# Attention logits with the features on the partitions: three banks of sums, a product with att two turns behind, edge features as 32 rows of 512

## The chip, the core and the metric

The program runs on one core of one Trainium2 chip. Its time is the device time of one execution in microseconds. Three executions of the kernel before took 2243.04, 2249.6 and 2248.37 us, a median of 2248.37 us. TensorE (PE) does the matrix products, VectorE (DVE) and ScalarE (ACT) work elementwise, GpSimd (POOL) issues gathers whose descriptors it makes itself, SyncE (SP) issues plain transfers.

## The reference, cut to what matters

Four graph layers follow each other over 3125 nodes with 128 features and 103,125 edges sorted by destination. The change touches the last one, an attention layer with 8 heads of 16 channels:

```python
x_l = (x @ W_l).reshape(n, H, C)
x_r = (x @ W_r).reshape(n, H, C)
e = (ea @ W_e).reshape(-1, H, C)
m = jax.nn.leaky_relu(x_l[src] + x_r[dst] + e, NEG_SLOPE)
alpha = jnp.einsum('ehc,hc->eh', m, att)
amax = jax.ops.segment_max(alpha, dst, num_segments=n)
expa = jnp.exp(alpha - amax[dst])
denom = jax.ops.segment_sum(expa, dst, num_segments=n)
a = expa / (denom[dst] + 1e-16)
out = jax.ops.segment_sum(x_l[src] * a[:, :, None], dst, num_segments=n)
```

For each edge there is a logit of each head: three rows of 128 are added, bent at zero (slope 0.2 below it), weighed with att and summed over the 16 channels of a head. Every node has a loop edge with itself, whose edge features are the mean.

## The kernel before, in words

The layer has three stages: `project` makes x_l (stored to memory, and gathered from there) and x_r (kept on chip as `xr`), `attention` goes over the edges, `feed_forward` normalizes and runs the two dense products. The change is in the first two.

`attention` takes the edges in 214 groups of 512 (four tiles of 128, edges on the partitions). There is one turn of the loop per group. The order on each engine is the order of the code; semaphores tie the engines.

- POOL: four gathers for each group (L2112), each of 128 rows of x_l by the edges' sources, into a ring of 28 groups. Before the gathers of group g it waits until group g-6 has been added up (`sums`), and until the ring's place is free.
- SP: two transfers of edge features per group, a broadcast of the destination numbers every second group, and per batch the marks of where nodes begin.
- PE, `logits(g)` (L2118): for each tile e = features times W_e, and x_r by a one-hot matrix `hot` that picks each edge's destination. A row is 136 wide: each head has a 17th column that holds 0.2 times the sum with att, so that the rest needs only max(z, 0) times 0.8 att. Four tiles stand in two banks; two groups take turns.
- DVE, per turn in this order: `one_hots(t+2)` (L2280), `add_rows(t)` (L2287: the sums from PE plus the gathered rows), `weigh(u)` (L2374), `bend(t)` (L2293), `add(u)` of the turn before (L2392), `head_sums(t)` (L2300: the sum over a head's 17 columns, which is alpha).
- A batch is up to 16 groups. When it is over, PE turns the alphas (`turn_alpha`, L2138) so that heads and groups are the partitions and the edges run along the row; DVE scans them for the maximum per node in both directions (L2308), a short chain carries the ends between groups, and the exponentials are turned back as weights.
- From 22 turns behind, group u is summed: DVE multiplies the gathered rows by the weights (`weigh`, output `both`), ACT makes `node_hot` (L2237, L2240), PE multiplies the two (`sum_rows`, L2180), DVE adds the sum into `acc` at a block given by a register. At the end of the loop there are two such groups in some turns, to catch up. At a batch's first group `spread_fall` (L2361, L2362, L2364) makes three short operations ahead of `weigh`.
- In the turns 0 to 4 DVE also computes the loop edges' logits (`own_logits`, L2399), 5 blocks of nodes at a time.

## Time and profile before

| | us |
|---|---|
| median of three runs (lowest, highest) | 2248.37 (2243.04, 2249.6) |
| span of the profiled execution | 2249.7 |
| attention, from the first gather at 984.64 to the last operations near 2187.5 | about 1203 |
| of it gathers, first start 984.64 to last start 2141.25 | 1156.6 |
| after the last gather to the end of attention | about 45 |
| feed_forward | about 62 |

The profile gives the profiled execution's span alone, no time around it; that span lies at the upper end of the three runs, 1.3 us over their median. Busy times over the whole span are PE 1665.0 us (74%), DVE 1504.7 (67%), ACT 969.8 (43%), POOL 916.3 (41%). TensorE's granted clock averages 0.829 of full speed. The share of an engine over the whole span mixes stages: POOL's 41% is nearly all in attention. An operation's row gives its start, its length, the engine, the line, output and inputs; a bracket behind it says how long the engine was idle before it, and what ended that. "issue" stands for idle time for which the profile shows nothing that was waited for.

### The profile page before, as it was taken

What the parts mean: (1) busy time and instruction counts of PE and PEld (TensorE: products, weight loads), DVE (VectorE), ACT (ScalarE), POOL (GpSimd) and SP (SyncE); (2) the same over time, 40 slices, a digit from 0 to 9 for tenths busy, and PEclk for the clock granted to TensorE, in tenths of its full rate; (3) what the DMA queues carried; (4) which work ended last, traced back from release to release, by engine and by line L of the source; (5) the groups of instructions that cost most, each with busy time, mean ns of one, the idle gap of its engine ahead of it and who ended that gap; (6) DMA issues with size and microseconds to landing.
All of it is one profiled execution on the core that took longest, in us unless ns stands there. A gap on an engine that the chain in (4) does not pass through costs nothing. (4 is left out here: it accounts for less than half of the span.)

```text
span 2249.7 us, 34161 instructions
## 1 busy us (share of the span) xinstructions
PE 1665.0 (74%) x10041; PEld 1359.7 (60%) x10041; DVE 1504.7 (67%) x3141; ACT 969.8 (43%) x2263; POOL 916.3 (41%) x880
## 2 busy tenths in 40 slices
PE   5566666899799999865667677766777767776756
PEld 2455555655478887634566666666666656666744
DVE  4766666577744342477677777867777867787875
ACT  0355565677455234430234434434434335344535
POOL 1000000000100000037777777777777777777800
PEclk9555555799999999988788988888888898898877
DMA  2100000000034000034333333333343333333211
GB/s 70 60 1 1 1 1 1 8 0 0 29 87 130 27 1 6 14 100 96 92 90 91 97 93 91 92 96 92 87 100 94 86 95 97 91 93 93 60 39 29
DMA packets 134433, 136.86 MB, mean 61 GB/s; under 512 B 28689, under 2 KB 105074, under 8 KB 134258
## 3 DMA queue, kind: packets, MB, share of 16 engines
q0 software_dynamic: 27776, 60.71, 12.2%
q1 hardware_dynamic: 106482, 73.98, 11.5%
q8 instruction: 90, 1.47, 0.3%
q14 instruction: 85, 0.70, 0.1%
HBM read 129.67 MB, written 4.92 MB: 60 GB/s over the span
## 5 line engine op out<-in xcount | busy, mean ns | idle before, releaser
L2112 POOL DMA_INDIRECT rows<-x_l,src x856 | 896.9, 1048 | 292.5 <-issue 260.1
L2180 PE MATMUL psum<-both,node_hot 128*128 128x144 f32 x1712 | 304.1, 332 | 202.0 <-DVE both L2374 175.2
L2180 PEld LDWEIGHTS psum<-both,node_hot 128*128 128x128 f32 x1712 | 264.7, 222 | 229.4 <-issue 197.4
L2127 PE MATMUL psum<-w_e,edges 128*128 128x272 f32 x856 | 323.9, 466 | 56.7 <-DVE z L2287 46.9
L2129 PEld LDWEIGHTS psum<-x_r,hot 128*128 128x128 f32 x1712 | 313.8, 224 | 51.1
L2129 PE MATMUL psum<-x_r,hot 128*128 x1712 | 313.1, 312 | 0.0
L2287 DVE TENSOR_TENSOR z<-psum,rows 128x544 f32<-128x544 f32 x214 | 154.3, 721 | 235.4 <-issue 163.7
L2237 ACT ACTIVATE apart<-iota,minus_rel 128x128 f32<-128x128 f32 x828 | 261.9, 386 | 0.0
L769 ACT ACTIVATE counts<-psum (+1 forms) x181 | 181.5, 1003 | 175.8 <-PE psum L762 112.1
L1145 POOL TENSOR_TENSOR ht<-ht,mix_rows 128x512 f32<-128x512 f32 (+1 forms) x7 | 7.8, 1149 | 587.4 <-ACT mix_rows L1186 587.4
L1260 PE MATMUL psum<-halves,counts 128*128 128x257 f16 (+1 forms) x1725 | 198.1, 277 | 7.4 <-DVE halves L1465 3.9
L762 PE MATMUL psum<-keys,x 128*128 128x125 f16 x1431 | 201.3, 283 | 0.4
L2127 PEld LDWEIGHTS psum<-w_e,edges 128*128 128x128 f32 x856 | 160.7, 228 | 62.4 <-DVE hot L2280 31.2
L1260 PEld LDWEIGHTS psum<-halves,counts 128*128 128x128 f16 (+1 forms) x1725 | 171.2, 100 | 34.3 <-DVE halves L1465 4.5
L725 DVE TENSOR_TENSOR x<-low_table,c_low 128x2048 f16<-128x2048 f16 x90 | 109.6, 1218 | 116.0 <-PE psum L762 114.6
L762 PEld LDWEIGHTS psum<-keys,x 128*128 128x128 f16 x1431 | 148.3, 104 | 25.8 <-issue 1.6
L2392 DVE TENSOR_TENSOR acc<-acc,psum 128x144 f32 x428 | 128.6, 300 | 44.9 <-PE psum L2180 8.0
L2233 ACT ACTIVATE both<-weight 128x64 f32<-128x64 f32 x214 | 52.9, 247 | 235.7 <-PE psum L2180 232.8
L2300 DVE TENSOR_REDUCE alpha<-z 128x32 f32<-128x544 f32 x214 | 152.5, 713 | 1.5 <-issue 0.3
L2293 DVE SCALAR_TENSOR_TENSOR z<-z,att 128x512 f32<-128x512 f32 x214 | 146.5, 685 | 1.1
L2374 DVE TENSOR_TENSOR both<-rows,weight 128x512 f32<-128x512 f32 x214 | 143.9, 680 | 0.2 <-ACT weight L2224 0.2
L740 PE MATMUL psum<-none 128*128 128x1 f16 x366 | 57.1, 183 | 105.7 <-ACT counts L769 102.1
(335 smaller groups left out, 2187.3 us busy)
## 6 DMA issues: line engine op xcount, KB each, us to landing
rel_row<-e_rel_rows SPq DMA_DIRECT2D x107, 256.0 KB
edges<-edge_t SPq DMA_DIRECT2D x428, 32.0 KB
rows<-x_l,src POOLq DMA_INDIRECT x856
edge_part<-edge_t SPq DMA_DIRECT2D x40, 320.0 KB, 3.1
x_r<-x_l SPq DMA_DIRECT2D x1, 1632.0 KB
ht<-x SPq DMA_DIRECT2D x6, 256.0 KB, 2.8
new<-e_new_before SPq DMA_DIRECT2D x12, 128.0 KB
new<-e_new_behind SPq DMA_DIRECT2D x12, 128.0 KB
```

The costliest lines, as they stand in the source:

```text
L762: last = e.matmul(flat[:, bass.ds(place[i - j * STRIDE], cols)], lows[hot], keys[hot], start=False, stop=True, skip_group_check=True)
L769: return e.activation(counts[:, :, column].rearrange("p h (a j) -> p h a j", j=w), pair.rearrange("p b (a n) -> p (b a) n", n=SLOT)[:, 0:f ...
L1260: last = e.matmul(ps, counts[:, i, b * P:b * P + rows], halves[:, i, :], start=i == 0, stop=i == s.nb - 1)
L2112: e.indirect_dma_start(rows[:, g % ring, j * ROW:(j + 1) * ROW], None, k.xl, bass.IndirectOffsetOnAxis(ap=src[:, at:at + 1], axis=0)).then ...
L2127: e.matmul(pair[:, j // 2, :], edges[:, r, :], w_e[:, j:j + 2, :].rearrange("p j f -> p (j f)"), start=True, stop=False)
L2129: final = e.matmul(pair[:, j // 2, j % 2 * ROW:(j % 2 + 1) * ROW], hot[:, two, j * P:(j + 1) * P], node_rows[j // 2], start=False, stop=j ...
L2180: final = e.matmul(to, near_hot[:, at, j, :], both[:, at, j, :], start=j % 2 == 0, stop=j % 2 == 1)
L2237: e.activation(apart[:, u % 2, j, :], iota[:, :], ACT.Abs, bias=minus_rel[:, 4 * u + j:4 * u + j + 1]).then_inc(*far.up())
L2287: e.tensor_tensor(z[:, g % 2, :].rearrange("p (b f) -> p b f", b=2), pair_of(g), rows_at(g).rearrange("p (b f) -> p b f", b=2), ALU.add).t ...
L2293: e.scalar_tensor_tensor(heads, heads, 0.0, att_of(k, 4), ALU.max, ALU.mult).then_inc(*leaky.up())
L2300: e.tensor_reduce(alpha[:, b.two, :, g - b.first, :], z[:, g % 2, :].rearrange("p (v h c) -> p v h c", v=4, h=HEADS), AX.X, ALU.add).then_ ...
L2374: e.tensor_tensor(both[:, at, :, 0:D].rearrange("p v (h c) -> p v h c", c=CH), rows_at(u).rearrange("p (v h c) -> p v h c", v=4, h=HEADS)[ ...
```

## The change

Within `attention`, the sums are built transposed: features on the partitions, the group's 512 edges along the row, in one bank per group, with three banks in turn (0, 1, 4).

- A row is 128 wide; the 17th columns go, and with them the products that filled them in `project`.
- PE, `begin(g)`: x_r of a block, split into three bf16 parts whose sum is x_r, times the bf16 one-hot matrix (three products of 256 columns for each of the group's two blocks), then W_e (32 x 128) times the edge features (32 rows of 512), one product of 512 columns. `join(g)`: the gathered rows of each tile times the identity, 4 of 128 columns, which adds them transposed. `head_sums(g)`: the bent sums times `att_heads` (att spread over the heads' columns), 512 columns, which gives the alphas with lines on the partitions at once; each group adds its 8 lines into the batch's bank (2 or 3). It runs two turns behind `join` (one at a batch's last group). `turn_alpha` is gone.
- ACT, `slope(g)`: 0.2 times the sums from the bank into `bent`.
- DVE, `bend(g)`: the maximum of the bank and `bent`. `add_rows` and DVE's `head_sums` are gone. `bend` stands behind `add`.
- The bf16 parts of x_r are made by POOL for the first 5 blocks, in `project`, and by DVE for the other 20 in the turns 0 to 3 (four operations for each 5 blocks). `own_logits` moves to the turns 5 to 9 and has one operation more; `add_bias` moves to the turns 10 to 19.
- SP: the edge features of a group go to 32 partitions, in three places instead of six; for group g SP waits for the products of group g-3. Two small loads more, and one smaller one in another form, stand in the tables' loads in `project`; one column more is loaded ahead.
- `hot` and `apart` are bf16.

```diff
-ROW = HEADS * (CH + 1)
+ROW = D
+LINES = 16 * HEADS
...
+                e.memset(k.att_heads[:, :], 0.0).then_inc(*blank.up())
+                e.wait_ge(kept_r.sem, kept_r.at(5))
+                row_parts.split(e, 0, split)
...
+                e.tensor_scalar(k.att_heads[:, LINES - HEADS:LINES], head_of[:, :], cols[:, 2:3], None, ALU.mult).then_inc(*v.up())
...
+class RowParts:
+
+
+    def __init__(self, k, scope, xr, rest):
+        s = k.s
+        self.xr, self.parts = xr, k.sb(scope, "x_r_parts", [P, s.nb, 3, D], BF16)
+        self.rest = rest.rearrange("p (b f) -> p b f", f=D)
+
+    def split(self, e, c, done):
+
+        at, rest = slice(5 * c, 5 * c + 5), self.rest
+        part = [self.parts[:, at, q, :] for q in range(3)]
+        if done.n:
+            e.wait_ge(done.sem, done.at(done.n))
+        e.tensor_copy(part[0], self.xr[:, at, :]).then_inc(*done.up())
+        t = done.n
+        e.wait_ge(done.sem, done.at(t))
+        e.tensor_tensor(rest[:, :, :], self.xr[:, at, :], part[0], ALU.subtract).then_inc(*done.up())
+        t = done.n
+        e.wait_ge(done.sem, done.at(t))
+        e.tensor_copy(part[1], rest[:, :, :]).then_inc(*done.up())
+        t = done.n
+        e.wait_ge(done.sem, done.at(t))
+        e.tensor_tensor(part[2], rest[:, :, :], part[1], ALU.subtract).then_inc(*done.up())
...
-    ring, slots, ahead, deep, lag = RING, 6, 4, 4, 22
+    ring, slots, edge_slots, deep, lag = RING, 6, 3, 4, 22
...
-        edges = sb("edges", [P, slots, P])
-        rel_row, hot = sb("rel_row", [P, slots, 4 * P], I16), sb("hot", [P, 2, 4 * P])
-        z, alpha = sb("z", [P, 2, 4 * ROW]), sb("alpha", [P, 2, 4, 16, HEADS])
+        edges = sb("edges", [DE, edge_slots, 4 * P])
+        rel_row, hot = sb("rel_row", [P, slots, 4 * P], I16), sb("hot", [P, 2, 4 * P], BF16)
+        bent = sb("bent", [P, 3, 4 * P])
...
-        turn_bank, misc = k.bank[4], k.bank[5]
+        split = k.flag("x_r_split")
+        z_banks, misc = (k.bank[0], k.bank[1], k.bank[4]), k.bank[5]
+
+        def summed_in(t):
+
+            ends = [b.over - 1 for b in plan]
+            return [g for g in (t - 2, t - 1) if 0 <= g < groups and (g == t - 1) == (g in ends)]
...
+        def bank_of(b):
+            return k.bank[2 + b.two]
+
+        def alphas_of(b):
+            return bank_of(b)[0:b.lines, :]
...
-                    if old >= 0:
-                        e.wait_ge(products.sem, products.at(old + 1))
+                    if g >= edge_slots:
+                        e.wait_ge(products.sem, products.at(g - edge_slots + 1))
                     for j, at in enumerate(two):
-                        e.dma_start(edges[j * P // 2:(j + 1) * P // 2, r, :], pairs_t[bass.ds(at, 1), :, :]
-                                                    .rearrange("o r e -> (o r) e")).then_inc(*edge_here[r].up(16))
+                        e.dma_start(edges[:, g % edge_slots, j * 2 * P:(j + 1) * 2 * P].rearrange("d (t e) -> d t e", t=2),
+                                    rows_of_pair(at)).then_inc(*edge_here[g % edge_slots].up(16))
...
-                        e.wait_ge(sums.sem, sums.at(g - slots + 1))
+                        e.wait_ge(joined.sem, joined.at(g - slots + 1))
...
-                def logits(g):
-                    r, two, pair = g % slots, g % 2, pair_of(g)
-                    node_rows = [xr[:, bass.ds(block_of.at(2 * g + j), 1), :].rearrange("p o f -> p (o f)") for j in range(2)]
+                def begin(g):
+                    two, z = g % 2, z_banks[g % 3]
+                    blocks = [block_of.at(2 * g + j) for j in range(2)]
+                    due_parts = min(2 * g + 1, s.nb - 1) // 5
+                    if due_parts > min(max(2 * g - 1, 0), s.nb - 1) // 5:
+                        e.wait_ge(split.sem, split.at(4 * due_parts))
                     e.wait_ge(hots.sem, hots.at(g + 1))
-                    e.wait_ge(edge_here[r].sem, edge_here[r].at(2 * lap(g)))
-                    if g >= 2:
-                        e.wait_ge(sums.sem, sums.at(g - 1))
+                    if g >= 3:
+                        e.wait_ge(leaky.sem, leaky.at(g - 2))
+                    for j in range(2):
+                        half = slice(j * 2 * P, (j + 1) * 2 * P)
+                        for q in range(3):
+                            e.matmul(z[:, half], row_parts.parts[:, bass.ds(blocks[j], 1), q, :].rearrange("p o f -> p (o f)"),
+                                     hot[:, two, half], start=j + q == 0, stop=False)
+                    e.wait_ge(edge_here[g % edge_slots].sem, edge_here[g % edge_slots].at(edge_lap(g)))
+                    e.matmul(z, w_e[:, :], edges[:, g % edge_slots, :], start=False, stop=False).then_inc(*products.up())
+
+                def join(g):
+                    z = z_banks[g % 3]
+                    e.wait_ge(got[g % slots].sem, got[g % slots].at(4 * lap(g)))
                     for j in range(4):
-                        if j % 2 == 0:
-                            e.matmul(pair[:, j // 2, :], edges[:, r, :], w_e[:, j:j + 2, :].rearrange("p j f -> p (j f)"),
-                                     start=True, stop=False)
-                        final = e.matmul(pair[:, j // 2, j % 2 * ROW:(j % 2 + 1) * ROW], hot[:, two, j * P:(j + 1) * P],
-                                         node_rows[j // 2], start=False, stop=j % 2 == 1)
-                    final.then_inc(*products.up())
-
-                def turn_alpha(b):
-                    e.wait_ge(alphas.sem, alphas.at(b.over))
+                        final = e.matmul(z[:, j * P:(j + 1) * P], rows_at(g)[:, j * P:(j + 1) * P], k.ident[:, :],
+                                         start=False, stop=j == 3)
+                    final.then_inc(*joined.up())
+
+                def head_sums(g):
+                    b = batch_of(g)
+                    c = g - b.first
+                    low = LINES - HEADS - c * HEADS
+                    e.wait_ge(leaky.sem, leaky.at(g + 1))
+                    if c == 0 and b.i >= 2:
+                        e.wait_ge(weights.sem, weights.at(2 * (b.i - 1)))
+                    e.matmul(alphas_of(b), k.att_heads[:, low:low + b.lines], bent[:, g % 3, :],
+                             start=c == 0, stop=c == b.n - 1).then_inc(*alphas.up())
...
-                logits(0)
+                begin(0)
                 for t in range(len(due)):
+                    if t < groups:
+                        join(t)
+                    for g in summed_in(t):
+                        head_sums(g)
                     if t + 1 < groups:
-                        logits(t + 1)
-                    for piece, turn in ((0, turn_alpha), (1, turn_ends), (2, turn_carries), (5, turn_weights)):
+                        begin(t + 1)
+                    for piece, turn in ((1, turn_ends), (2, turn_carries), (5, turn_weights)):
...
+                def slope(g):
+                    e.wait_ge(joined.sem, joined.at(g + 1))
+                    if g >= 3:
+                        e.wait_ge(alphas.sem, alphas.at(g - 2))
+                    e.activation(bent[:, g % 3, :], z_banks[g % 3], ACT.Copy, scale=NEG_SLOPE).then_inc(*sloped.up())
...
+                        slope(t)
...
-                def add_rows(g):
-                    e.wait_ge(products.sem, products.at(g + 1))
-                    e.wait_ge(got[g % slots].sem, got[g % slots].at(4 * lap(g)))
-                    if g >= 2:
-                        e.wait_ge(alphas.sem, alphas.at(g - 1))
-                    e.tensor_tensor(z[:, g % 2, :].rearrange("p (b f) -> p b f", b=2), pair_of(g),
-                                            rows_at(g).rearrange("p (b f) -> p b f", b=2), ALU.add).then_inc(*sums.up())
-
                 def bend(g):
-                    heads = z[:, g % 2, :].rearrange("p (v h c) -> p v h c", v=4, h=HEADS)[:, :, :, 0:CH]
-                    e.wait_ge(sums.sem, sums.at(g + 1))
-                    e.scalar_tensor_tensor(heads, heads, 0.0, att_of(k, 4), ALU.max, ALU.mult).then_inc(*leaky.up())
-
-                def head_sums(g):
-                    b = batch_of(g)
-                    e.wait_ge(leaky.sem, leaky.at(g + 1))
-                    if b.i >= 2:
-                        e.wait_ge(turned.sem, turned.at(4 * (b.i - 1)))
-                    e.tensor_reduce(alpha[:, b.two, :, g - b.first, :], z[:, g % 2, :].rearrange(
-                        "p (v h c) -> p v h c", v=4, h=HEADS), AX.X, ALU.add).then_inc(*alphas.up())
...
-                        add_rows(t)
                     for u in due[t]:
                         if u in begun:
                             spread_fall(begun[u])
                         weigh(u)
-                    if t < groups:
-                        bend(t)
                     for u in due[t - 1] if t else []:
                         add(u)
                     if t < groups:
-                        head_sums(t)
-                    if t < cuts:
-                        own_logits(t)
-                    if cuts <= t < 3 * cuts:
-                        add_bias(t - cuts)
+                        bend(t)
+                    if t + 1 < cuts:
+                        row_parts.split(e, t + 1, split)
+                    if cuts <= t < 2 * cuts:
+                        own_logits(t - cuts)
+                    if 2 * cuts <= t < 4 * cuts:
+                        add_bias(t - 2 * cuts)```

What now stands on the engines can be read from the compiled order. On DVE, in the middle of the loop, a turn was this before (from the one-hot matrix of a group two ahead, to the next turn's one):

```order
L2280 TENSOR_SCALAR hot<-rel_row,place 128x512
L2287 TENSOR_TENSOR z<-psum,rows 128x544
L2374 TENSOR_TENSOR both<-rows,weight 128x4x128
L2293 SCALAR_TENSOR_TENSOR z<-z,att 128x32x16
L2392 ISA
L2392 TENSOR_TENSOR acc<-acc,psum 128x144
L2392 ISA
L2392 TENSOR_TENSOR acc<-acc,psum 128x144
L2300 TENSOR_REDUCE alpha<-z 128x4x8
```

The same turn on DVE in the changed kernel (2349 is `hot`, 2426 `weigh`, 2444 `add`, 2353 `bend`):

```order
L2349 TENSOR_SCALAR hot<-rel_row,place 128x512
L2426 TENSOR_TENSOR both<-rows,weight 128x4x128
L2444 ISA
L2444 TENSOR_TENSOR acc<-acc,psum 128x144
L2444 ISA
L2444 TENSOR_TENSOR acc<-acc,psum 128x144
L2353 TENSOR_TENSOR bent<-psum,bent 128x512
```

Two operations of the turn are gone. `hot` now stands directly ahead of `both`, and `both` is followed by the additions into `acc`; the bend reads a bank of sums and stands last.

On PE, in the middle of the loop, this is a turn before, `logits` and `sum_rows`:

```order
L2127 MATMUL psum<-w_e,edges 128x272
L2129 ISA
L2129 MATMUL psum<-x_r,hot 128x136 x2
L2127 MATMUL psum<-w_e,edges 128x272
L2129 ISA
L2129 MATMUL psum<-x_r,hot 128x136 x2
L2180 MATMUL psum<-both,node_hot 128x144 x4
```

And in the changed kernel: `join`, `head_sums`, then `begin` with six pairs like the first two rows here, of which the last two pairs are shown, and `sum_rows`, then the next turn's `join` and `head_sums`:

```order
L2174 ISA
L2174 MATMUL psum<-hot,x_r_parts 128x256
L2174 ISA
L2174 MATMUL psum<-hot,x_r_parts 128x256
L2177 MATMUL psum<-edges,w_e 128x512
L2240 MATMUL psum<-both,node_hot 128x144 x4
L2183 MATMUL psum<-ident,rows 128x128 x4
L2194 MATMUL psum<-bent,att_heads 128x512
```

The wait for the gathered rows has moved from DVE's L2287 to PE's L2183, which heads PE's turn.

## Rows read from the trace of the kernel before

**Rows 1.** Busy time in four stretches: the stretch, then each engine; clock, DMA last

```profile
core 0: us, PE busy (x) PEld busy (x) DVE busy (x) ACT busy (x) POOL busy (x), PEclk, DMA share, GB/s
985.00:1110.00 125.00, 73.67 (x304) 60.92 (x304) 90.47 (x140) 7.42 (x20) 96.95 (x93) 0.76 0.41 100
1110.00:1900.00 790.00, 559.77 (x3119) 497.66 (x3120) 589.83 (x1196) 322.98 (x968) 610.09 (x591) 0.87 0.38 93
1900.00:2143.00 243.00, 177.07 (x1024) 158.29 (x1024) 197.50 (x404) 108.67 (x331) 189.46 (x174) 0.87 0.36 89
2143.00:2188.00 45.00, 26.09 (x137) 23.21 (x136) 33.62 (x94) 17.42 (x60) 0.00 (x0) 0.73 0.06 13
```

**Rows 2.** Attention, groups of instructions: count, busy us, mean ns, idle before

```profile
L2112 POOL DMA_INDIRECT rows<-x_l,src x856 | 896.9, 1048 | 292.5 <-issue 260.1 <-DMA x_l<-rows 31.8 <-DVE both L2374 0.6
L2127 PE MATMUL psum<-w_e,edges 128*128 128x272 f32 x856 | 323.9, 466 | 56.7 <-DVE z L2287 46.9 <-DVE hot L2280 9.8
...
L2287 DVE TENSOR_TENSOR z<-psum,rows 128x544 f32<-128x544 f32 x214 | 154.3, 721 | 235.4 <-issue 163.7 <-PE psum L2129 69.4 <-DMA rows<-x_l,src 2.1
L2300 DVE TENSOR_REDUCE alpha<-z 128x32 f32<-128x544 f32 x214 | 152.5, 713 | 1.5 <-issue 0.3
L2293 DVE SCALAR_TENSOR_TENSOR z<-z,att 128x512 f32<-128x512 f32 x214 | 146.5, 685 | 1.1
L2374 DVE TENSOR_TENSOR both<-rows,weight 128x512 f32<-128x512 f32 x214 | 143.9, 680 | 0.2 <-ACT weight L2224 0.2
L2392 DVE TENSOR_TENSOR acc<-acc,psum 128x144 f32 x428 | 128.6, 300 | 44.9 <-PE psum L2180 8.0 <-DVE acc L2392 5.9
...
L2280 DVE TENSOR_SCALAR hot<-rel_row,place 128x512 f32<-128x512 int16 x214 | 104.2, 487 | 5.3 <-PE psum L2129 4.4 <-DMA rel_row<-e_rel_rows 0.9
...
L2224 ACT ACTIVATE weight<-psum 128x512 f32<-128x512 f32 x24 | 13.0, 594 | 6.9 <-PE psum L2160 5.9 <-PE psum L2157 1.0
...
L2347 DVE TENSOR_TENSOR trial<-psum,trial 128x512 f32<-128x512 f32 x12 | 8.3, 691 | 0.4
```

**Rows 3.** The gathers' line: count, shortest/median/longest in ns, first and last start

```profile
L2112 POOL DMA_INDIRECT rows<-x_l,src x856: 940/947/3946, 984.6 to 2141.2; - x172
```

**Rows 4.** In order of time, around 1552 to 1562 us: start, length, engine, operation

```profile
1552.89 0.62 PE L2127 MATMUL psum<-w_e,edges 128*128 128x272 f32 x2
...
1553.35 0.63 PE L2129 MATMUL psum<-x_r,hot 128*128 x4
...
1556.07 0.68 DVE L2374 TENSOR_TENSOR both<-rows,weight 128x512 f32<-128x512 f32 x1
...
1556.57 1.00 POOL L2112 DMA_INDIRECT rows<-x_l,src  x1 [0.31 <-issue]
1556.67 0.68 DVE L2293 SCALAR_TENSOR_TENSOR z<-z,att 128x512 f32<-128x512 f32 x1
...
1561.56 0.68 DVE L2374 TENSOR_TENSOR both<-rows,weight 128x512 f32<-128x512 f32 x1
...
1561.76 1.30 POOL L2112 DMA_INDIRECT rows<-x_l,src  x1 [0.30 <-issue]
```

**Rows 5.** In order of time, first and last of the 18 longest gathers

```profile
1112.22 0.27 DVE L2364 TENSOR_SCALAR factor<-mask,fall 8x136 f32<-8x136 f32 x1
1112.26 2.27 POOL L2112 DMA_INDIRECT rows<-x_l,src  x1 [0.30 <-issue]
1112.42 0.67 DVE L2374 TENSOR_TENSOR both<-rows,weight 128x512 f32<-128x512 f32 x1
1113.03 0.67 DVE L2293 SCALAR_TENSOR_TENSOR z<-z,att 128x512 f32<-128x512 f32 x1
...
2136.99 3.95 POOL L2112 DMA_INDIRECT rows<-x_l,src  x1 [0.30 <-issue]
```

**Rows 6.** The page's row of the fp16 products of an earlier layer

```profile
L1260 PE MATMUL psum<-halves,counts 128*128 128x257 f16 (+1 forms) x1725 | 198.1, 277 | 7.4 <-DVE halves L1465 3.9
```

141 lines of the change are left out of this document (74 added, 67 removed).

## The prediction

> **What bounds the kernel now.** I read the stretches first, then the groups of attention, then the gathers alone, and last the order of time around some of them. The change lies in attention, 1203 of 2249.7 us. There no arithmetic engine is full: in the middle stretch of 790 us DVE is busy 590, PE 560 at a granted clock of 0.87, ACT 323 [rows 1]. POOL shows 610, but between its gathers stands a gap of 0.30 us that waits for nothing the profile shows (292.5 us idle, of it 31.8 before the first gather and 0.6 for DVE) [rows 2]. Gather and gap together leave it no free time: 591 gathers in 790 us are 1.337 us each. DVE's `add_rows` is idle 235 us before it, mostly "issue" and 69 for PE [rows 2]: it is late because its rows are. So POOL's row of gathers sets the stage. The change keeps all 856.
>
> A gather's median is 0.947 us, its mean 1.048 [rows 2, 3]. With the gap of 0.304, 856 undisturbed ones take 1071 us; what lies over it is 896.9 - 856 x 0.947 = 86 us. That excess is what the change can act on. Its cause shows in the order of time. The gather at 1561.76 starts 0.20 us into `both` and lasts 1.30 (0.35 over); the one at 1556.57 starts 0.50 into it and lasts 1.00 (0.05 over) [rows 4]. Both are late by what was left of about 0.6 us of that DVE operation, and both get in although another such operation follows it at once. Beside a string that begins with short tensor_scalar operations it is worse: the gather at 1112.26 was held until `bend` ended at 1113.70, 1.33 us over, and the last long one took 3.95 [rows 5]. Of such long ones, over 1.2 us too much, there are 18, 29.6 us in all.
>
> **The change part by part.** *Excess of the gathers, before.* An operation that reads two tensors in SBUF and holds a gather about 0.6 us costs, with gathers 1.35 us apart, 0.6/1.35 x 0.3 = 0.135 us a turn, 29 us in 214 turns. `both` and `bend` are two of them; `hot` (487 ns, about 0.4 of it effective) comes to 0.4/1.35 x 0.2 = 0.06, 13 us. The 15 strings at a batch's first group are near 1.3 each, 20 us. The sum of 91 stands against 86 measured; I scale the single operations to 66/71, 0.93.
>
> *Excess after.* `bend` reads a bank of sums and one tensor in SBUF, as `add_rows` does now, so its 27 us go. In the 15 strings `bend` falls off the end: 0.6 each, -9. `hot` writes two bytes instead of four; between no gain and half its length that is 0 to -7, I take -3. Against it, `hot` now stands directly ahead of `both`. If a gather that starts in `hot` is held through `both` as at 1112.26, 0.3/1.35 x 0.6 = 0.133 us a turn, 28 us, come back; if not, nothing. The row nearest in kind (tensor_scalar, then `both`) says that it is held; but the gathers in rows 4 slip in between two operations back to back. I take half, +14. The splitting of x_r and the longer `own_logits` are 13 operations more with two SBUF operands or casts of 640 elements in the turns 0 to 9: each about 0.8/1.35 x 0.4 = 0.24, +3. Sum: -27 - 9 - 3 + 14 + 3 = -22 us, between -39 (not held, `hot` halved) and -5 (held, `hot` as long as now).
>
> The Trainium skill's page "SBUF — State Buffer" (Who interferes with whom) says that an operation with two SBUF inputs contends only with a GpSimd instruction that reads SBUF, and that making descriptors needs the write side, so that a tensor_tensor should not stall it; only the two-port modes of tensor_scalar and copies should. That speaks against the gain. The trace disagrees on the first half: `both` is a tensor_tensor and the gathers in [rows 4] are late by its rest. By the page alone removing `bend` is worth nothing and the time stays where it is.
>
> *PE.* A product of 272 fp32 columns is followed 0.46 us later by the next [rows 4]: 1.69 ns a column at full clock, twice that at half. Before, a turn has 1088 + 576 columns, 2.81 us. After, fp32: 512 for W_e, 512 for `join`, 512 for `head_sums`, 576 for `sum_rows`, 3.57 us; 16-bit: 1536 columns at 198.1/1725/257 = 0.45 ns [rows 6], 0.69 us. Together 4.26, with the batch's transposes about 4.35, in a turn of 1156.6/214 = 5.40 us. At full clock PE is 80% busy, at 0.87 92%. It still fits, so I cost it at nothing; the cover is POOL's own pace. Should PE fall behind, POOL waits only when it is six groups ahead of `join`, so single late turns are hidden.
>
> *DVE.* It loses 721 + 713 ns and has `bend` at 691 (the form of L2347) for 685, and a shorter `hot`: from 3.9 to about 2.4 us of a turn [rows 2]. It was not the bound, so this brings nothing by itself.
>
> *ACT.* It gets `slope`, 594 ns as L2224 [rows 2], on 323/790 x 5.4 = 2.2 us a turn [rows 1]. `slope` stands behind the next group's `node_hot` (and in a batch's fifth turn behind the wait for the turned weights), and `bend`, then the next `weigh`, stand behind it on DVE; PE's `sum_rows` waits for that. This delays a turn or two a batch by a few us, within the six groups.
>
> *Queues.* SP issues as many transfers for a group as now, three groups ahead of their use, about 16 us. The rows gathered are 6% shorter; transfers are busy 0.38, so nothing. The two loads more in `project` and POOL's four operations there lie beside DVE's and ACT's work, ahead of POOL's 31.8 us wait for x_l [rows 2]: 0, at most +2. Behind the last gather, `add_rows`, `bend` and `head_sums` of 721 + 685 + 713 ns become `join` 0.87, `slope` 0.59, `bend` 0.69 and the product 0.87; DVE's adds no longer wait behind the gathered rows. 0, give or take 2.
>
> The sum on the profiled execution is 2249.7 - 22 = 2228, and 1.3 less, 2227, on the median's scale.
>
> **The rivals.** *PE becomes the bound (slower).* Place: PE's turn of 4.35 us at full clock. It decides from a granted clock of 4.35/5.40 = 0.81 down, since then POOL's six groups fill up. For it: the clock was 0.76 in the first stretch, 0.87 later [rows 1]. Against it: PE was 59% busy at 0.76 and 71% at 0.87 [rows 1], so the higher clock went with the busier PE, and it will be busier still. If it averaged 0.77 over 192 turns, a turn takes 5.65, +0.25 each, +48 us: 2297.
>
> *The strings catch a gather every turn (slower).* Each turn of DVE is tied to the landing of the turn's rows, and so to a gather's start: `hot` and `both` stand at a fixed place against the gathers. If that place is on a start, a gather is held up to 0.9 us instead of my mean of about 0.3, in every other turn at least, since the delay moves the next string away: about 0.45 x 214 = 96 us of excess, with the rest 110 against 86: +22, 2271.
>
> *They catch none (faster).* The same tie, the place between two starts: only the 15 strings and the first turns stay, 15 to 20 us of excess: -68, 2181. For it: `hot` and `both` are 0.9 of 1.25 us, so a quarter of the places are free.
>
> *No change.* The gathers' excess is not DVE's doing, or all of `bend` comes back through `hot`: 2242 to 2255. This is the page's case too.
>
> **How the numbers follow.** Forecast (2212 to 2241): 0.43. None caught, or nearly (below 2212): 0.14. No change: 0.19. PE the bound: 0.12. Caught in every other turn: 0.12. Faster by over 0.3% (6.7 us, what a measurement of this kernel can tell) 0.57, within it 0.19, slower 0.24. The range leaves out the free extreme and PE's full price: 2194 to 2264; the forecast's own is 2212 to 2241.
>
> **What would show it.** The gathers' mean falls from 1048 to near 1020 ns, median and gap unchanged, and they stay back to back; late ones start inside `hot` or `both`, none inside `bend`. The long ones fall to about 0.9 over. PE is busy some 80% of the stretch at a clock above 0.9. The forecast is wrong if POOL's idle time is ended by PE's `join`, if the turn is no longer 4 gathers, or if the mean stays at 1048.

## The result and the profile after

The changed kernel takes 2238.9 us median (2235.3 to 2243.4, 13 runs) where the kernel before takes 2244.7 (2240.3 to 2254.3): ratio 0.9968, 95% interval 0.9958 to 0.9977. A second measurement (r_after below) gave 0.9968 again (0.9955 to 0.9981). That is 0.3% faster, 5.8 us where some 21 were forecast. The time lies within the prediction's range, 12 us above its forecast of 2227, and the gain is as small as its "no change" had it. It is not right for that: the gathers gained more than twice what was forecast, an order of operations that was costed at nothing lost most of it again, and the two nearly cancel.

The first three stretches after, as in [rows 1] (the third ends 13 us earlier here, where the gathers have long been done):

```profile
core 0: us, PE busy (x) PEld busy (x) DVE busy (x) ACT busy (x) POOL busy (x), PEclk, DMA share, GB/s
985.00:1110.00 125.00, 101.07 (x429) 57.26 (x430) 73.48 (x117) 18.74 (x37) 95.62 (x96) 0.85 0.35 93
1110.00:1900.00 790.00, 749.24 (x4123) 491.87 (x4124) 415.43 (x935) 412.42 (x1154) 603.76 (x612) 0.99 0.35 93
1900.00:2130.00 230.00, 205.37 (x1126) 139.06 (x1124) 127.11 (x292) 119.33 (x344) 148.80 (x150) 0.93 0.29 78
```

PE is busy 749 of 790 us, 95%, where it was 560, and its granted clock rose from 0.87 to 0.99. POOL issues 612 gathers in the middle stretch where it issued 591.

The gathers' own row, to be laid beside [rows 3]: count, shortest, median and longest in ns, first and last start.

```profile
L2156 POOL DMA_INDIRECT rows<-x_l,src x856: 940/944/3127, 985.4 to 2092.4; - x172
```

The last gather starts at 2092.4 instead of 2141.2: 49 us earlier. The span is only 15 us shorter. The page's rows of the changed operations, as in [rows 2], say where the rest is:

```profile
L2156 POOL DMA_INDIRECT rows<-x_l,src x856 | 848.2, 991 | 278.7 <-issue 253.3
L2353 DVE TENSOR_TENSOR bent<-psum,bent 128x512 f32<-128x512 f32 x214 | 147.7, 690 | 315.3 <-ACT bent L2280 315.0
L2280 ACT ACTIVATE bent<-psum 128x512 f32<-128x512 f32 x214 | 126.4, 591 | 398.5 <-PE psum L2183 376.2
L2349 DVE TENSOR_SCALAR hot<-rel_row,place 128x512 bf16<-128x512 int16 x214 | 77.8, 364 | 141.8 <-PE psum L2177 112.7
```

DVE's `bend` waits 315 us for ACT's `slope`. In the middle turns that costs nothing: `bend` mostly starts 4.3 to 6.5 us after the fourth gather of its group, which is the landing and TensorE's `join`, and where it is later it catches up within the batch. At the end it doesn't catch up. Read from the timeline this lag is 7.4 us at turn 180, 15.4 at 181, 16.4 at 190, 9.2 at 196, 15.8 at 197, 21.8 at 204, 28.8 at 208 and 42.6 at 213. In the kernel before the last `z` starts at 2146.49, 5.2 us behind the last gather. So 49 us were won by the gathers, 37 were lost between the last gather and the last `bend`, and 4 were won after it: 15.

One such place, in order of time (start, length, engine, operation; in brackets the wait):

```profile
2080.68 1.16 PE L2183 MATMUL psum<-ident,rows 128*128 128x128 f32 x8
...
2085.18 1.10 PE L2183 MATMUL psum<-ident,rows 128*128 128x128 f32 x8
2085.19 0.77 ACT L2294 ACTIVATE weight<-psum 128x320 f32<-128x320 f32 x2 [3.60 <-PE psum L2220]
2086.05 0.26 ACT L2303 ACTIVATE both<-weight 128x64 f32<-128x64 f32 x1
2086.21 1.26 ACT L2307 ACTIVATE apart<-iota,rel 128x128 bf16<-128x128 f32 x4
...
2087.50 0.63 ACT L2310 ACTIVATE node_hot<-apart 128x512 f32<-128x512 bf16 x1
2088.04 0.24 ACT L2303 ACTIVATE both<-weight 128x64 f32<-128x64 f32 x1
2088.18 1.26 ACT L2307 ACTIVATE apart<-iota,rel 128x128 bf16<-128x128 f32 x4
...
2089.48 0.63 ACT L2310 ACTIVATE node_hot<-apart 128x512 f32<-128x512 bf16 x1
...
2090.01 0.58 ACT L2280 ACTIVATE bent<-psum 128x512 f32<-128x512 f32 x1
...
2090.62 0.69 DVE L2353 TENSOR_TENSOR bent<-psum,bent 128x512 f32<-128x512 f32 x1 [9.01 <-ACT bent L2280]
...
2091.37 1.94 PE L2194 MATMUL psum<-bent,att_heads 128*48 128x512 f32 x2 [4.10 <-DVE bent L2353]
...
2098.10 1.05 PE L2183 MATMUL psum<-ident,rows 128*128 128x128 f32 x8
```

This is turn 207, the fifth after a batch's end. `join` is done at 2081.8. ACT waits 3.6 us for the turned weights and copies them at 2085.2 (`keep_weights`), then prepares the two groups that are summed in the next turn (`fill`, 2.0 us each), and only then comes `slope`, at 2090.0, 8.2 us late. DVE stands still for it for 9.0 us, and then TensorE for 4. The engine that now has the least to spare is held up by one that is half idle. From the `join` of turn 208 (2085.18) to that of turn 209 (2098.10) it takes 12.9 us.

Such turns are few. Where a turn has two groups to sum but nothing of a batch's end, `slope` is 2.1 us late, TensorE has no gap, and its turn takes 5.62 us, for example from 1958.66 to 1964.27:

```profile
1958.66 1.05 PE L2183 MATMUL psum<-ident,rows 128*128 128x128 f32 x8
...
1962.21 2.23 PE L2240 MATMUL psum<-both,node_hot 128*128 128x144 f32 x16
1964.27 1.05 PE L2183 MATMUL psum<-ident,rows 128*128 128x128 f32 x8
```

The time is lost two turns behind those in which ACT also waits for a batch's ends or weights. From one `join` to the next it is 10.5 us up to turn 183, 12.2 up to 199, 13.1 up to 205, 12.9 up to 209 and 13.2 up to 211, 62.0 us in all.

### The profile page after: what moved, and what is told of

Its sections match the earlier page's. It is cut to its first block and busy times, and to the rows that moved or that the text cites. A ratio compares the mean times of both kernels' runs of the same rounds, so it can differ in the third digit from the quotient of the medians.

```text
span 2234.5 us, 37102 instructions
## 1 busy us (share of the span) xinstructions
PE 1911.7 (86%) x11265; PEld 1332.3 (60%) x11265; DVE 1236.5 (55%) x2729; ACT 1080.3 (48%) x2477; POOL 871.6 (39%) x884
## 5 line engine op out<-in xcount | busy, mean ns | idle before, releaser
L2156 POOL DMA_INDIRECT rows<-x_l,src x856 | 848.2, 991 | 278.7 <-issue 253.3
L2353 DVE TENSOR_TENSOR bent<-psum,bent 128x512 f32<-128x512 f32 x214 | 147.7, 690 | 315.3 <-ACT bent L2280 315.0
L2280 ACT ACTIVATE bent<-psum 128x512 f32<-128x512 f32 x214 | 126.4, 591 | 398.5 <-PE psum L2183 376.2
L2240 PEld LDWEIGHTS psum<-both,node_hot 128*128 128x128 f32 x1712 | 233.4, 200 | 108.0 <-issue 102.1
L2183 PE MATMUL psum<-ident,rows 128*128 128x128 f32 x1712 | 245.8, 289 | 40.4 <-DMA rows<-x_l,src 39.0
L2240 PE MATMUL psum<-both,node_hot 128*128 128x144 f32 x1712 | 271.9, 307 | 2.8 <-DVE acc L2444 2.1
L2183 PEld LDWEIGHTS psum<-ident,rows 128*128 128x128 f32 x1712 | 218.9, 199 | 75.2 <-DMA rows<-x_l,src 66.0
L2307 ACT ACTIVATE apart<-iota,rel 128x128 bf16<-128x128 f32 x828 | 262.3, 388 | 0.1
L2177 PE MATMUL psum<-edges,w_e 32*128 32x512 f32 x428 | 242.1, 645 | 0.0
L2194 PE MATMUL psum<-bent,att_heads 128*128 128x512 f32 (+2 forms) x428 | 226.2, 616 | 7.4 <-DVE bent L2353 7.4
L2174 PEld LDWEIGHTS psum<-hot,x_r_parts 128*128 x1284 | 127.3, 100 | 140.7 <-issue 129.3
L2174 PE MATMUL psum<-hot,x_r_parts 128*128 128x256 bf16 x1284 | 179.5, 277 | 8.8 <-DVE hot L2349 8.8
L2444 DVE TENSOR_TENSOR acc<-acc,psum 128x144 f32 x428 | 129.1, 302 | 76.6 <-PE psum L2240 39.4
L2349 DVE TENSOR_SCALAR hot<-rel_row,place 128x512 bf16<-128x512 int16 x214 | 77.8, 364 | 141.8 <-PE psum L2177 112.7
```

The source lines that it names most:

```text
L2156: e.indirect_dma_start(rows[:, g % ring, j * ROW:(j + 1) * ROW], None, k.xl, bass.IndirectOffsetOnAxis(ap=src[:, at:at + 1], axis=0)).then ...
L2174: e.matmul(z[:, half], row_parts.parts[:, bass.ds(blocks[j], 1), q, :].rearrange("p o f -> p (o f)"), hot[:, two, half], start=j + q == 0, ...
L2177: e.matmul(z, w_e[:, :], edges[:, g % edge_slots, :], start=False, stop=False).then_inc(*products.up())
L2183: final = e.matmul(z[:, j * P:(j + 1) * P], rows_at(g)[:, j * P:(j + 1) * P], k.ident[:, :], start=False, stop=j == 3)
L2194: e.matmul(alphas_of(b), k.att_heads[:, low:low + b.lines], bent[:, g % 3, :], start=c == 0, stop=c == b.n - 1).then_inc(*alphas.up())
L2240: final = e.matmul(to, near_hot[:, at, j, :], both[:, at, j, :], start=j % 2 == 0, stop=j % 2 == 1)
```

## The experiments

Two theories stood after the traces. **A:** ACT's order. `slope` stands behind the fills, and where a turn has two of them everything behind `slope` is late. **P:** TensorE's turn. It was read as 5.07 us where 4.26 were estimated (4.63 without a wait, below), more with a second `sum_rows`, against POOL's 5.17, so TensorE sets the late turns. The ratios are to the kernel before on the same chip. The runs r_ and t_ were on chips where the kernel before takes 2244 to 2246 us; the runs e_ and s_ came on chips where it takes 2515, and are told last.

**r_slope_first: slope ahead of everything in ACT's turn**

```
                 for t in range(len(due)):
+                    if t < groups:
+                        slope(t)
                     b = batch_at(t, 1)
...
                         fill(u)
-                    if t < groups:
-                        slope(t)
```

> The changed kernel with slope(t) moved to the head of ACT's turn, ahead of the next groups' fills. Theory A (ACT's order: two fills of 2.0 us each ahead of slope delay bend and all behind it in the turns with two sum_rows, where 34 us of the 49 won by the gathers are lost): 20 to 34 us under r_after, and bend starts no more than 15 us behind the last gather. Theory P (TensorE's turn of 5.0 us, 6.3 with a second sum_rows, sets those turns): within 6 us of r_after, and bend still starts some 35 to 43 us behind the last gather.

Measured 2196.1 us (2195.3 to 2199.9), ratio 0.9779 (0.9759 to 0.9799), beside the unedited kernel:

> The changed kernel itself, unedited, as the reference for the three kernels beside it. All theories: a ratio to the kernel before near 0.997 if this chip's granted clock is about 0.88 over the run; if the clock of the kernel before is again only 0.78, the ratio should be near 0.96, as for the three edited kernels that ran on such a chip, since before loses more there.

It took 2238.1 (2235.1 to 2240.8), ratio 0.9968. The edit is worth 42 us. Two rows of its trace, first the gathers, then the same place in the same turn as above:

```profile
L2156 POOL DMA_INDIRECT rows<-x_l,src x856: 943/947/3104, 982.7 to 2090.4; - x172
```

```profile
2059.55 1.16 PE L2183 MATMUL psum<-ident,rows 128*128 128x128 f32 x8
...
2060.74 0.60 ACT L2280 ACTIVATE bent<-psum 128x512 f32<-128x512 f32 x1 [0.29 <-PE psum L2183]
2061.37 0.69 DVE L2353 TENSOR_TENSOR bent<-psum,bent 128x512 f32<-128x512 f32 x1 [0.89 <-ACT bent L2280]
```

The last gather starts at 2090.4, 2 us earlier than in the first profile of the changed kernel and 5.5 earlier than in that of r_after. The last `bend` now follows it by 6.3 us instead of 42.6 (40.7 in r_after), and no turn's lag is over 12.0. `slope` and `bend` stand right behind `join`, and the five long turns of TensorE take 33.2 us together instead of 62.0. Theory A, and by more than its 20 to 34 us. The plain turns with two groups take 5.62 us with either order: there `slope` could be 2.1 us late at no cost.

**r_one_part and r_slope_one: one bf16 part of x_r instead of three**

```
-                        for q in range(3):
+                        for q in range(1):
```

> The changed kernel with one of the three bf16 parts of x_r multiplied by the one-hots (the two parts that carry the rest of x_r's precision are left out): TensorE's turn falls from 5.0 to about 4.2 us at full clock. Theory P: the last 46 turns get 46 x 0.8 = 37 us of TensorE back, so 25 to 37 us under r_after, and bend follows the last gather by under 15 us. Theory A: the fills still stand ahead of slope, at most 6 us under r_after. On a chip with a low clock both are blurred: 4.2 us at 0.9 against a gather turn of 5.2.

> Both edits at once: slope(t) at the head of ACT's turn and one of three bf16 parts. Theory P: as r_one_part within 5 us. Theory A: as r_slope_first within 5 us. If both are needed, because either TensorE or ACT holds the late turns once the other is freed: each alone gives under half of what the two give together, about 34 us.

Measured 2242.6 (2234.5 to 2249.5), ratio 0.998 (0.9964 to 0.9996); with slope first 2216.1 (2207.2 to 2222.2), 0.9872 (0.9849 to 0.9895). Four products fewer a turn bring nothing, and `bend` still follows the last gather by 36.6 us: theory P falls as the cause of the loss. The plain turns with two groups do become shorter (5.18 us instead of 5.62), so TensorE sets those, as P had it, but the five long turns take 63.2 us. Together with slope first the lighter kernel is even 20 us slower than slope first alone, which neither theory foresaw. The middle stretch, in this order r_slope_first and r_slope_one:

```profile
1110.00:1900.00 790.00, 759.61 (x4160) 493.62 (x4159) 426.30 (x936) 416.60 (x1155) 601.22 (x619) 1.00 0.35 94
```

```profile
1110.00:1900.00 790.00, 701.98 (x3507) 437.57 (x3506) 421.65 (x927) 411.93 (x1143) 604.34 (x610) 0.98 0.35 93
```

POOL issues 610 gathers instead of 619 and the clock is lower (0.873 to 0.879 over whole runs, against 0.886 to 0.890). More gathers start inside `both` (112 against 67, 28.5 us of excess against 17.0). The two profiled runs differ by 8 us, and by chance they are the slowest of the one kernel and the fastest of the other; the medians differ by 20, and what holds the rest is open.

**t_between: slope behind keep_weights, ahead of the fills**

```
                     if b:
                         keep_weights(b)
+                    if t < groups:
+                        slope(t)
                     for u in (due[t + 1] if t + 1 < len(due) else []):
                         fill(u)
-                    if t < groups:
-                        slope(t)
```

> The changed kernel with slope(t) behind keep_weights and ahead of the fills, on another chip than the first time. Judged against 0.9968 (the changed kernel) and 0.9779 (slope at the head) where the kernel before takes about 2245. If the fills made slope late: 0.978 to 0.981. If keep_weights' wait for the turned weights did: 0.993 or more. By the timeline of the changed kernel (join done at 2083.3, weights turned until 2087.4, two fills until 2091.4, then slope) each has half of the delay where they meet, but doubled fills are in some thirty turns and turned weights in fourteen, so 0.979 to 0.985. If this is a chip where before takes over 2400, it only says whether the row of waits before slope names PE's transposes still.

Measured 2198.5 (2195.8 to 2202.4), ratio 0.9787 (0.9774 to 0.9801): within 2.5 us of slope at the head. With the fills out of the way the wait for the turned weights costs nothing that can be measured: `slope` is still 4.0 to 4.3 us late in the turns 181, 197 and 207, and the five long turns take 35.2 us. That does not make the fills alone the cause. In the plain turns they made `slope` 2.1 us late and cost nothing; the loss came where one turn had both, a batch's wait and two fills, 6.1 to 8.4 us together. In the middle of the loop the wait and one fill, 6.4 us, were made good. A kernel with the fills ahead of `slope` and the wait behind it was not run.

**t_bend_bank: the kernel before, bend with one operand in SBUF**

It multiplies the bank of edge sums with the bias rows instead of z with att; the logits lose the gathered rows and att, the instruction keeps its size and its length (684 ns, 685 before). Since `bend` now reads the bank, PE waits for `bend` instead of `add_rows` before it writes there again.

```
-                        e.wait_ge(sums.sem, sums.at(g - 1))
+                        e.wait_ge(leaky.sem, leaky.at(g - 1))
...
-                    e.scalar_tensor_tensor(heads, heads, 0.0, att_of(k, 4), ALU.max, ALU.mult)
+                    e.scalar_tensor_tensor(part, pair_of(g)[:, :, 0:2 * D], 0.0, row, ALU.max, ALU.mult)
```

> The kernel before, with bend reading the bank of edge sums and the bias rows instead of z and att, as in the run where POOL was not the bound; there the 58 gathers that start inside bend cost 0.0 us. If the second SBUF operand is what holds them and POOL is back to back here: excess 89 to about 60, time 2245 - 25 = 2220 (ratio 0.985 to 0.993). If what the gathers gain is lost again behind them, as in the changed kernel: ratio 0.994 or more with the last gather's start some 25 us earlier.

Measured 2218.2 (2215.4 to 2220.1), ratio 0.9878 (0.9863 to 0.9893): 28 us. The gathers' row beside [rows 3]:

```profile
L2112 POOL DMA_INDIRECT rows<-x_l,src x856: 940/944/2577, 986.6 to 2105.4; - x172
```

The gathers' excess over 0.944 us each falls from 89 to 51. By the operation that DVE had started last when they start (of two that overlap by some 0.08 us, the later): inside `bend` from 14.9 us (71 gathers) to none (77 gathers); inside `z`, which `both` and then `bend` follow at once, from 10.7 (63) to 4.4 (72); inside `both` it nearly stays, 26.7 (121) and 24.8 (118); the long ones at the strings make the rest. The same string in the two kernels shows what `bend` does at its end, first before, then here. Both gathers start 0.5 us into `z`. The first is 1.29 us too long, which is until `bend` is over, the second 0.68, until `both` is:

```profile
1779.45 0.70 DVE L2287 TENSOR_TENSOR z<-psum,rows 128x544 f32<-128x544 f32 x1
1779.95 2.23 POOL L2112 DMA_INDIRECT rows<-x_l,src  x1 [0.31 <-issue]
1780.09 0.67 DVE L2374 TENSOR_TENSOR both<-rows,weight 128x512 f32<-128x512 f32 x1
1780.69 0.67 DVE L2293 SCALAR_TENSOR_TENSOR z<-z,att 128x512 f32<-128x512 f32 x1
```

```profile
1760.83 0.70 DVE L2287 TENSOR_TENSOR z<-psum,rows 128x544 f32<-128x544 f32 x1
1761.34 1.62 POOL L2112 DMA_INDIRECT rows<-x_l,src  x1 [0.30 <-issue]
1761.47 0.67 DVE L2375 TENSOR_TENSOR both<-rows,weight 128x512 f32<-128x512 f32 x1
1762.07 0.67 DVE L2294 SCALAR_TENSOR_TENSOR z<-psum,rows 128x512 f32<-128x512 f32 x1
```

**t_first_apart: slope first, and the one-hots away from both**

```
-                    if t + 2 < groups:
-                        one_hots(t + 2)
                     for u in due[t]:
...
                     for u in due[t - 1] if t else []:
                         add(u)
+                    if t + 2 < groups:
+                        one_hots(t + 2)
```

> Slope at the head of ACT's turn and one_hots(t + 2) behind the adds, again on another chip. Against 0.9779 for slope first alone, where before takes about 2245. If the chain hot, both holds gathers: 0.973 or less. If no chain forms: within 0.003 of 0.978; on the chip where transfers and the clock rule it was 0.9523 against 0.9576 of slope first (another call), a gain that the gathers' excess (37.4 us against 33.7) does not explain. If TensorE's products come late because the one-hots do: above 0.981.

Measured 2198.8 (2193.3 to 2199.9), ratio 0.9784 (0.9764 to 0.9804), as slope first alone. Taking the two apart brings nothing in time. The chain does exist. In the changed kernel's first profile 48 gathers start inside `hot`, 5.6 us of excess, and seven of them, held through `both`, make 5.0 of it; in r_after it is 48, 3.5 us and three; in r_slope_first 25 start there, 0.8 us, and none is held. One of the seven:

```profile
1848.78 0.34 DVE L2349 TENSOR_SCALAR hot<-rel_row,place 128x512 bf16<-128x512 int16 x1
1848.79 1.75 POOL L2156 DMA_INDIRECT rows<-x_l,src  x1 [0.30 <-issue]
1849.04 0.67 DVE L2426 TENSOR_TENSOR both<-rows,weight 128x512 f32<-128x512 f32 x1
```

**t_four_parts: slope first, and two products more**

```
-                        for q in range(3):
+                        for q in (0, 1, 2, 2):
```

> Slope at the head of ACT's turn and the third bf16 part multiplied twice, again on another chip: TensorE's turn 5.0 + 0.27 us against POOL's 5.17. If TensorE becomes the bound there: +0.1 to 0.2 us a turn, ratio 0.988 to 0.998, POOL waiting for join in the middle turns. If the batch's own waits leave room: within 0.003 of 0.978.

Measured 2206.5 (2201.7 to 2210.7), ratio 0.9825 (0.9803 to 0.9846): 10 us over slope first, between the two expectations. The six products of a turn take 0.75 us (below), so two more in 214 turns are 214 x 0.25 = 53 us, and four fifths of it are still covered: by this estimate TensorE's turn of 4.63 us becomes 4.88, and four undisturbed gathers take 4 x (0.944 + 0.304) = 4.99. POOL waits for `join` only seven times, 2.1 us in all, and its gathers take as long as with slope first alone. `bend` follows the last one by 12.9 us instead of 6.3, and the first gather starts 4 us later, which lies ahead of the edit. TensorE was near its limit, and still not the bound.

**The runs where the kernel before takes 2515 us.** Four kernels on one such chip:

> The changed kernel with ACT's slope(t) at the head of ACT's turn instead of behind the fills and the kept weights. Theory A (order): in the last 46 turns DVE's bend and PE's products wait for ACT, whose turn has up to two fills of 2.0 us ahead of slope; the last bend then comes less than 42.6 us behind the start of the last gather (I expect about 20 to 25), the gathers stay as they are (last start near 2092), and the time falls by 12 to 22 us against the changed kernel, to about 2220. Theory B (PE's work is the bound at the end, ACT only fills the wait): the lag stays 38 to 45 us and the time within 4 us of 2239.

> The changed kernel with only the first of the three bf16 parts of x_r multiplied (the sums leave out what the other two hold, and the work of making them stays): 4 products of 256 columns less on PE a turn, about 0.5 us of 5.0. Theory B (PE's work bounds the last part): 46 turns at 0.5 us are about 20 us, of which 15 to 25 come off the time, and the lag at the last gather falls to about 20. Theory A (ACT's order): PE waits for bend anyway, the time falls by under 8 us and the last bend stays over 35 us behind. In the middle, where the gathers set the pace at 5.0 us a turn, both expect no change.

> The kernel before with bend reading PE's bank and one row instead of the sums and att (512 elements as before; the logits then leave out the gathered rows, and att is replaced by the rows of the two biases). The operation stays in its place at about the same length, but reads one tensor in SBUF instead of two. Port theory: the gathers' excess over 0.945 us falls from 86 to 89 us by what bend holds (15 to 35 us), the last gather starts that much earlier than 2141, and the time falls by 15 to 30 us. Rival (a gather is late because DVE is busy, whatever it reads, or because of the number of DVE's operations): excess and time as before, within 6 us.

> The changed kernel with the one-hot matrix made behind weigh and add instead of directly ahead of both. My prediction cost that place at +14 us of gathers' excess. Chain theory: the excess of 38.5 us falls by about 14; against it the trace after shows only 5.6 us for the 48 gathers that start inside hot, so that without a chain it stays 33 to 42 us. The time changes little either way, within 5 us, because the last part is not bound by the gathers (both theories); if the time falls as the excess does, the gathers do bound the end.

The edits are those of r_slope_first, r_one_part and t_bend_bank, and that of the one-hots without slope first. Measured 2407.7, 2409.3, 2521.2 and 2446.7; ratios 0.9576 (0.9525 to 0.9626), 0.959 (0.9535 to 0.9644), 1.0026 (0.9997 to 1.0055), 0.9739 (0.9685 to 0.9793). The changed kernel itself was not among them, so they don't rank the edits against it. And POOL is not the bound there. For e3_bend_bank, POOL's waits between 1200 and 1900 us (waited for, us, times, longest), and TensorE's clock in 4-us windows:

```profile
POOL rows L2112 <- DVE both L2375: 160.8, 34, 7.0
POOL rows L2112 <- issue: 121.8, 386, 1.9
```

```profile
1524.00:1528.00 4.00, 0.76 (x5) 0.50 (x4) 1.24 (x3) 2.25 (x7) 3.06 (x4) 1.00 0.26 57
1528.00:1532.00 4.00, 0.00 (x0) 0.00 (x0) 0.54 (x2) 0.00 (x0) 0.95 (x1) 0.60 0.14 35
1532.00:1536.00 4.00, 2.68 (x10) 2.59 (x11) 3.86 (x8) 0.00 (x0) 1.77 (x2) 0.50 0.25 60
1536.00:1540.00 4.00, 4.00 (x21) 3.65 (x20) 2.75 (x7) 0.00 (x0) 3.09 (x4) 0.62 0.44 108
```

In the second row the engines stand still for some 3 us, TensorE for all 4 (it is idle from 1524.8 to 1533.4); its clock falls to the lower level (0.50, 1.2 GHz) and stays there while it works again. Such holes come every few turns, 34 of over 2.5 us between 1200 and 1900 us, and a gain of POOL's vanishes in them: in e3_bend_bank the gathers' excess is 46 us, nothing of it from the 53 that start inside `bend`, and its time did not move. No profile of the unedited kernel before was taken on such a chip, so its excess there is not known. What ends the holes the profile doesn't name plainly; the cause of the 270 us is open.

Four kernels more fell on another such chip (before 2515.7):

> The changed kernel with slope(t) behind keep_weights and ahead of the fills. It splits the 42 us that slope at the head of the turn brought against the changed kernel's 2238. If the fills (2.0 us each, two in the late turns) made slope late: about 2196 to 2202, as with slope at the head. If it was the wait of keep_weights for the transposes that TensorE makes behind the next group's products (4.2 us at a batch's fifth turn, 14 batches): the fills are small beside it and this stays within 10 us of 2238. I expect between: most of the late turns' gain, since the doubled turns are more than the batch turns, 2198 to 2212; the end of the last batches still late by a few us each.

> The changed kernel with slope(t) at the head of ACT's turn and one_hots(t + 2) moved on DVE from ahead of the product `both` to behind the adds, so that the two no longer follow each other. If the chain hot, both holds gathers (my step of +14 us, 0 to 28): 10 us or more under slope first alone (2196), with fewer late gathers inside `both`. If a 16-bit hot holds hardly any gather and no chain forms, as the excess by starting place says (51 gathers inside hot 3.8 us in all): within 5 us of 2196. Slower is possible, since begin(t+1) on TensorE gets its one-hots later: on the slow chip this move alone cost 37 us against slope first.

> The kernel before, whose bend reads the bank of edge sums and the bias rows instead of z and att (both in SBUF); the logits are then wrong in value, the instructions' sizes the same. One SBUF operand instead of two. If the second SBUF operand is what holds a gather that starts inside bend: the 71 gathers that cost 14.9 us there cost under 1, those inside z (held through the bend behind it) half of 10.8, and the long ones at the strings fall by 0.6 each; gathers' excess 89 to about 60, time 2245 - 25 = 2220 (2210 to 2230). If it is the write, or any long operation, the excess stays at 89 and the time within 3 us of before.

> Slope at the head of ACT's turn, and the third bf16 part multiplied twice: two products of 256 columns more a turn, 0.27 us on TensorE's 5.0. It asks how much of TensorE's cover is left against POOL's turn of 5.17 us. If TensorE is the bound from a turn of about 5.2 us on: +0.1 to +0.2 us in 200 turns and the batch's transposes on top, 2216 to 2240, POOL waiting for join. If there is still room: within 6 us of 2196.

The edits are those of t_between, t_first_apart, t_bend_bank and t_four_parts. Measured 2411.9, 2395.5, 2523.7 and 2427.0, ratios 0.9598 (0.9571 to 0.9624), 0.9523 (0.9496 to 0.955), 1.0034 (1.0017 to 1.0051), 0.9654 (0.963 to 0.9678). They settle none of the questions. One thing they show: there the one-hots' later place with slope first (0.9523) is better than slope between (0.9598), a difference that the other chips don't have.

## Why the prediction was right or wrong

**POOL's row of gathers bounds attention, its excess is DVE's doing: right for the kernel before.** t_bend_bank takes one SBUF operand from one operation and the kernel is 28 us faster. In the changed kernel it sets the pace of the middle, but no longer that of the end.

**Excess after, forecast -22: the way right, the size less than half.** The profiled excess fell from 89 to 40 us, and the last gather came 49 us earlier. By where the gathers start, with those over 1.2 us too long counted apart: long ones 29.6 to 2.2 us (18 and one), inside `bend` 14.9 to none, inside `both` 26.7 to 16.1 (121 and 56 gathers), inside `hot` 3.1 to 5.6, the rest 14.5 to 16.2 (forecast +3). So the strings' -9 was the mis-sized term: -27. The 11 us of `both` no term had, and why fewer gathers start there is not shown. `bend` -27: within it alone it was 15. With the strings' -9, which is `bend` at the end of a string, the forecast for its operand is -36; t_bend_bank measured -38 in the excess and -28 in time, so the total was right and its split was not, and that 27 and 28 agree is luck. Chain +14, the middle between a row that spoke for it and one that spoke against: 5.0 us in one profile, 2.1 in another, none in a third. `hot` -3: right (3.1 us to 0.6, the chain apart). Two slips of the working change nothing: the low end of the sum is -40, not -39, and 110 against 86 is +24, not +22.

**ACT, costed at nothing: the step that failed.** The prediction said that `slope` stands behind the next group's `node_hot`, that `bend` and PE's work stand behind it, and that "this delays a turn or two a batch by a few us, within the six groups". For the middle of the loop that held: `slope` is 6.4 us late in a batch's fifth turn there, and the lag is made good. I had looked at a turn with one fill, and did not lay the order against the schedule, which puts two groups into 21 turns between 182 and 212, where three batches also end. There the batch's wait and two fills together make `slope` up to 8.4 us late. The delay goes round through DVE and TensorE: `bend`, the next `weigh`, `sum_rows`, and `join` behind it. A turn with two groups takes TensorE 5.62 us, more than four gathers (about 5.0), so it has nothing to catch up with, and the six groups of cover are no help at the end, where no gather comes after. Measured: 42 us, between r_after and r_slope_first. In the profiles, -49 for the gathers' end, +37 for the lag behind it and -4 for the tail are the 15 us by which the spans differ; without the late `slope` the change would have been 2196, outside the forecast's own range on the fast side (2181 was the price of the case that no string catches a gather). That the measured 2238.9 lies in that range is luck.

**TensorE, costed at nothing: right, its turn mis-sized.** A turn of the changed kernel in which it waits for nothing, up to the next `join`:

```profile
1893.29 1.05 PE L2183 MATMUL psum<-ident,rows 128*128 128x128 f32 x8
1894.18 1.02 PE L2194 MATMUL psum<-bent,att_heads 128*128 128x512 f32 x2
1895.04 0.82 PE L2174 MATMUL psum<-hot,x_r_parts 128*128 128x256 bf16 x6
1895.79 1.12 PE L2177 MATMUL psum<-edges,w_e 32*128 32x512 f32 x2
1896.84 1.25 PE L2240 MATMUL psum<-both,node_hot 128*128 128x144 f32 x8
1897.92 1.05 PE L2183 MATMUL psum<-ident,rows 128*128 128x128 f32 x8
```

The starts lie 0.89, 0.86, 0.75, 1.05 and 1.08 us apart, 4.63 in all. Columns alone gave 0.87, 0.87, 0.69, 0.87 and 0.97. `join` and `head_sums` fit; the products of 32 rows by 512 carry 0.18 more, those of 128 by 144 0.11, the 16-bit ones 0.06. (The 5.07 us above are from the `join` at 1551.09 to that at 1556.16, with the wait for the gathered rows in them.) The rival "PE becomes the bound" had its point of decision at a clock of 0.81; with the turn as measured it is 4.63/5.17 = 0.90. It didn't come true since the clock rose to 0.99: the argument from [rows 1], that the busier engine had the higher clock, held, and r_one_part shows it from the other side (0.95 and 709 us busy in the middle stretch, against 0.98 and 750 in r_after). In the turns with two groups TensorE does set the pace.

**The case of the Trainium skill's page.** The Trainium skill's "SBUF — State Buffer" (Who interferes with whom) would have a tensor_tensor leave the making of descriptors alone. The trace and t_bend_bank disagree: gathers that start inside `both`, a tensor_tensor with two SBUF inputs, are late by up to its rest, or through the operation behind it too, and taking the second SBUF input from `bend` ended its part. The Trainium skill's page marks that remark on descriptors as inferred. Its rule in the same section that an operation with two SBUF inputs contends with a GpSimd instruction that reads SBUF agrees with all this if the gather counts as one; its source numbers `src` lie in SBUF. Whether it is that read which is held, no run shows.

**The tail, 0 give or take 2:** from the last `bend` to the end it is 99.5 us, from the last `z` 103.2. **Queues and project, 0 to +2:** POOL waits for no other transfer than before, and the first gather starts 0.8 us later. DVE's `hot` now waits 29.1 us in all for its row of destination numbers (0.9 before); what that costs was not separated. **The signs:** the gathers' mean is 991 ns where 1020 was expected, PE is busy 95% instead of 80%, the clock is above 0.9, no gather is late inside `bend`, and PE's `join` ends only 2.7 us of POOL's idle time.

## What to carry to other kernels

Where a schedule puts double work into some turns, cost an added instruction in the fullest turn, not in the common one, and in each engine's order of issue: what it stands behind can become its price. One delay alone may be free, as 2.1 us a turn were here; ask where two of them meet, and whether any turn after that has time to spare. A short operation on which two other engines wait belongs at the head of its engine's turn; here that made 2196.1 us, the fastest of all kernels run, 2.2% under the kernel before. And where one engine's queue sets a stage, count what its neighbours do while it starts: where one operand of one operation lies was worth 28 us, more than the 22 of the whole forecast.

## What the runs showed of the hardware

- Two operations of 512 fp32 columns on DVE of the same length hold POOL's gathers quite differently: with two inputs in SBUF, 71 starts cost 14.9 us; with one in PSUM, 77 starts cost nothing (`bend` before, and in t_bend_bank). A 16-bit `hot` with one input costs 0.8 us in 25 starts in r_slope_first and 5.6 in 48 in the changed kernel, 5.0 of it from seven that were held through the `both` behind it.
- Less work on TensorE went with a lower granted clock and no shorter time: one part of three, 0.854 to 0.869 over a whole run against 0.874 to 0.881.
- Chips differ by 12% on the same kernel (2245 and 2515 us), and on the slower ones other waits rule: the change is worth 0.3% on the one kind, while on the other, where the change itself was not run, all edits of it are 2.6 to 4.8% under the kernel before.
